# Weighing two score groups at once: eight passes in a row, with a ring of four groups of exponentials

## The chip, the cores and the metric

One core of one Trainium2 chip runs the kernel. The metric is the device time of one execution in microseconds (us). The kernel before took 2647.45 us (median of 3 runs, 2641.01 to 2655.77).

## The reference

The input is x, 8 batches of 1024 tokens with 512 features, all in float32. One layer is computed:

```python
Q, K, V = x @ W_Q.T, x @ W_K.T, x @ W_V.T            # 16 heads of 32 features
attn = where(causal, einsum('bhqd,bhkd->bhqk', Q, K) / sqrt(32), -inf)
y = einsum('bhqk,bhkd->bhqd', softmax(attn), V) @ W_O.T
x = layernorm(x + y)
p = softmax(x @ router_w.T + router_b)               # 8 experts
out = (x @ expert_w[argmax p].T + expert_b[argmax p]) * max(p)
x = layernorm(x + out)
```

## The kernel before, in words

**Stages.** `split_weights` splits the weights and the first batch of x into a high and a low part (fp32r), so that a product can be made of three passes. `attend` then does eight batches: seven in a hardware loop, the last one written out again. `run_experts` gathers the routed rows tile by tile and applies the experts. The change lies in `attend` alone.

**A batch.** An opening makes queries and keys of unit 1 and the row maxima of unit 0. Then come four units `u` of four heads each; a unit has 12 score groups `j` (`SCORE_GROUPS`), numbered through the batch as `n = 12 u + j`. A group is one block of 128 keys against one half (`BANK` = 512) of the queries, for four heads. Groups 0 to 3 belong to the first half and groups 4 to 11 to the second; because of the causal mask their widths are 512, 384, 256, 128 and 512 five times, 384, 256, 128 columns. Groups 0 to 3 and 8 to 11 lie on the diagonal. A closing makes the output products, the first layer norm, the routing, and queries, keys and values of the next batch.

**A group on each engine.** TensorE writes one score tile for each head (line 1009) into a ring of PSUM banks: 2 banks in units 0 and 1, 3 in unit 2, 4 in unit 3 (`score_bank`). ScalarE takes the exponential of each tile (line 697) into the SBUF ring `probs`, of `PROBS` = 3 groups. On the diagonal GpSimd zeroes the masked part (line 568). TensorE then weighs the group: `weigh(n, False)` multiplies it with the values into `y_ps`, `weigh(n, True)` with ones into `den_ps`, the sums. A weighing is four matmuls with 32 columns of weights, one for each head, side by side in the array by `tile_position`; each of them is two records in the trace, so that a weighing of a group is two passes over its columns, and both weighings together four passes. `weigh(n, True)` counts `probs_used`, which frees the slot of the ring. Below, a burst is a run of such passes between two full-width matmuls.

**The order on TensorE** is written out by hand, from line 1085 on. In each group the four score tiles stand with, between them, the row-maximum tiles of the next unit (`max_tile`, line 997; up to group 9 in unit 0, up to group 8 in units 1 and 2) and, in units 0 and 1, thirds of a projection for the unit after the next (line 951). Right after the second score tile of group n, group n - 2 (`LAG` = 2) is weighed:

```python
if n >= LAG and h == 1:
    weigh(n - LAG, False)
    weigh(n - LAG, True)
```

The last two groups of a batch are weighed after the loop. In unit 3 an output product of 12 matmuls follows groups 8, 9 and 10. `transpose_max` (line 1040) turns the finished maxima at the end of group 10 in unit 0 and of group 9 in units 1 and 2; ScalarE negates them and sends them by DMA into the query stack, where the score tiles of the next unit read them.

**VectorE** reduces the maximum tiles (lines 751 and 757) from a ring of three banks (four in unit 0's own opening), makes the low parts of projections, and copies `y_ps` and `den_ps` out when a half of a unit is weighed (`copy_y`, line 782, and `turn_sums`, line 790, at groups 2 and 6 of the unit).

**SyncE's queue** (`one_pass` of `block.sync`) issues the DMAs in a fixed order, each behind the waits of those before. `send(b, u)` sends the parts of unit u to its stacks and behind each of queries and keys loads the `w_qk` weights of the unit after (line 435). `load_xt(b + 1, 0)` and `(b + 1, 1)`, the first two parts of the next batch of x into `xt_raw` (line 439), are issued early in the batch, before `send(b, 2)`. ScalarE reads them in unit 2 (`split_high`, line 629, at groups 1, 3, 5, 7); GpSimd makes the low parts (`split_low`, line 525, at groups 4, 4, 6, 11), and parts 2 and 3 are loaded only when parts 0 and 1 have been split. In the closing `xt_raw` serves again, as `x_in`, for the residual (`load_x`, line 462).

Of the kernel before, what the change touches and what calls it, by code (L numbers as in the profile page):

```python
# [43 lines left out]
SETS = 3  # L44
PROBS = 3
LAG = PROBS - 1
WO_SET, WV_SET = 1, 2
# [101 lines left out]
def attend(nc, region_end, xt, xt_raw, x_t, x_rows, router_w_t, router_b, w_qk_parts, w_vo, dispatched):  # L149

    with ExitStack() as ctx:
# [11 lines left out]


        w_qk = sb("w_qk", [P, 2, 2, KT, P], F32R)
        q_st = [sb(f"q_stack{s}", [P, 4, SEQ], F32R) for s in range(SETS)]
        k_st = [sb(f"k_stack{s}", [P, 4, SEQ], F32R) for s in range(SETS)]
        v = sb("v", [P, ROWT, D])
        parts = sb("parts", [P, 2, 2, BANK], F32R)
        probs = sb("probs", [P, 4 * PROBS, BANK])  # L170
        rows = sb("rows", [P, ROWT, ROW])
# [165 lines left out]
        def weighed(eng, b, n):  # L337

            eng.wait_ge(probs_used.sem, probs_used.at(b, n))

        def scored(eng, b, n):

            eng.wait_ge(exp_done.sem, exp_done.at(b, 4 * n))
# [86 lines left out]
        def _(sp):  # L430
# [14 lines left out]
            def send(b, u):  # L445
                for o in (Q, K):
                    for t in range(HALVES):
                        send_tile(sp, b, u, o, t, range(SP_BLOCKS), sp_in, held_sp)
                    if not (u == UNITS - 1 and isinstance(b, int)):
                        load_w((u + 1) % UNITS, o)  # L450

# [7 lines left out]
            def one_pass(b, last):  # L459
# [10 lines left out]
                hold(sp, held_sp)  # L470
                for k in range(0 if last else 2):
                    load_xt(b + 1, k)
                wait_job(sp, b, proj_full, ("v", 6))
# [7 lines left out]
                send(b, 3)  # L481
                hold(sp, held_sp)
                scored(sp, b, GROUPS * 2)
                hold(sp, held_sp)
# [18 lines left out]
                for tb in range(2, ROWT):  # L503
                    wait_job(sp, b, proj_free, ("o", tb - 2))
                    load_x(tb)
                if not last:
                    send(b, 0)
# [6 lines left out]
        def _(pool):  # L514
# [43 lines left out]
            def one_pass(b, last):  # L558
                def keep_causal(u, j):

                    t, kb = SCORE_GROUPS[j]
                    n = GROUPS * u + j
                    c = column(kb, t)
                    for h in (0, 2):
                        pool.wait_ge(exp_done.sem, exp_done.at(b, 4 * n + h + 2))
                        hold(pool, held_pool)
                        block = probs[:, 4 * (n % PROBS) + h:4 * (n % PROBS) + h + 2, c:c + P]
                        nc.gpsimd.affine_select(out=block, in_=block, compare_op=ALU.is_ge, fill=0.0, base=0,  # L568
                                                pattern=[[0, 2], [1, P]], channel_multiplier=-1)\
                            .then_inc(probs_masked.sem, 1)  # L570
# [55 lines left out]
        def _(act):  # L626
# [25 lines left out]
            def one_pass(b, last):  # L652
# [29 lines left out]
                for u in range(UNITS):  # L682
                    for j, (t, kb) in enumerate(SCORE_GROUPS):
# [10 lines left out]
                        for h in range(4):  # L694
                            c = column(kb, t)
                            act.wait_ge(score_full.sem, score_full.at(b, 4 * n + h + 1))
                            nc.scalar.activation(probs[:, 4 * (n % PROBS) + h, c:BANK], score_bank(u, 4 * j + h)[:, c:BANK],  # L697
                                                 ACT.Exp, scale=SCALE).then_inc(exp_done.sem, 1)
                            if u + 2 < UNITS and h == 1:
                                for i in tiles_made(j):  # L700
                                    high(b, u + 2, i)
# [225 lines left out]
        def _(pe):  # L927
# [50 lines left out]
            def one_pass(b, last):  # L978
# [34 lines left out]
                def weigh(n, sums_too):  # L1013
# [13 lines left out]
                    for h in range(4):  # L1027
                        head = 4 * u + h
                        mm = nc.tensor.matmul((den_ps if sums_too else y_ps)[DH * h:DH * (h + 1), c:BANK],  # L1029
                                              ones_f[:, :] if sums_too else v[:, kb, head * DH:(head + 1) * DH],  # L1030
                                              probs[:, 4 * (n % PROBS) + h, c:BANK], start=kb == 0, stop=last,
                                              tile_position=(0, DH * h), skip_group_check=True)
                    if sums_too:
                        mm.then_inc(probs_used.sem, 1)

                def transpose_max(u):
# [52 lines left out]
                for u in range(UNITS):  # L1089
                    for j in range(GROUPS):  # L1090
# [8 lines left out]
                        for h in range(4):  # L1099
                            for i in share(maxed, h):  # L1100
                                max_tile(u + 1, i)
                            score_tile(u, j, h)
                            if h % 2 == 0:
                                for p in made[h // 2:h // 2 + 1]:
                                    project(b, u + 2, p // 3, third(p % 3))
                            if n >= LAG and h == 1:
                                weigh(n - LAG, False)
                                weigh(n - LAG, True)
                        if u == 0 and j == 0:
# [7 lines left out]
                        if u + 1 < UNITS and j == MAX_GROUPS[u > 0][1]:  # L1117
                            transpose_max(u + 1)
                for n in range(UNITS * GROUPS - LAG, UNITS * GROUPS):
                    weigh(n, False)  # L1120
                    weigh(n, True)

# [400 lines left out]
```

## Time and profile before

| what | value |
|---|---|
| median of 3 runs | 2647.45 us |
| the profiled execution | 2662.11 us |
| its span (first to last instruction) | 2660.4 us |
| mean granted TensorE clock | 0.964 of full speed |
| TensorE matmul busy | 2400.2 us, 90% |
| VectorE / ScalarE / GpSimd busy | 1451.5 / 1019.4 / 877.3 us |

The durations below come from the profiled execution; the median of the runs is 14.7 us under its time. Times of a row are microseconds from the start of its span. All rows of a stretch come from the fourth batch, whose unit 0 begins at 969.44, unit 1 at 1022.44, unit 2 at 1074.48 and unit 3 at 1119.25. A group's time is that from its first score matmul to the next group's.

### The profile page before, as it was taken

The page shows a single profiled execution, that of the slowest core. Times are in us where ns is not written, and L with a number is a line of the kernel's source. Part 1 is how long each engine was busy: PE and PEld are TensorE (multiplying, and loading weights), DVE is VectorE, ACT ScalarE, POOL GpSimd, SP SyncE. Part 2 cuts the span into 40 slices and gives each one's busy share as a digit, 9 for nine tenths or more (in the row PEclk, how much of TensorE's full clock was granted, in tenths as well). Part 3 has the DMA queues.
Part 4 walks back from the last instruction along what each step waited for, and adds up shares of the span by engine and source line. Part 5 has one row for each costly group of instructions (what it writes and reads, how often), then busy time and mean ns, then how long its engine had stood idle before and what let it go on. Part 6 is the DMA issues. An engine that isn't in the chain of part 4 may idle for free. (4 is left out here: it accounts for less than half of the span.)

```text
span 2660.4 us, 51133 instructions
## 1 busy us (share of the span) xinstructions
PE 2400.2 (90%) x14336; PEld 1534.2 (58%) x14337; DVE 1451.5 (55%) x3931; ACT 1019.4 (38%) x2089; POOL 877.3 (33%) x1531
## 2 busy tenths in 40 slices
PE   2999989999999989998999999999999899809998
PEld 1654665557554755476545755476547654607886
DVE  2576356734664367535663557437653675336665
ACT  2245414551345224531454144523452245223333
POOL 2222332323223232323223323232332322234656
PEclk9999999999999999998999999999999999859999
DMA  8432153314431253215231443134322421054443
GB/s 295 134 90 74 64 151 94 108 57 125 123 97 61 74 160 78 101 46 157 76 99 61 134 110 101 64 117 127 88 73 72 144 73 48 25 196 142 147 148 122
DMA packets 131032, 283.03 MB, mean 106 GB/s; under 512 B 33026, under 2 KB 42242, under 8 KB 128452
## 3 DMA queue, kind: packets, MB, share of 16 engines
q1 hardware_dynamic: 100920, 208.62, 26.0%
q0 software_dynamic: 28304, 70.64, 9.0%
q8 instruction: 124, 2.03, 0.3%
q14 instruction: 148, 1.21, 0.1%
q10 hardware_dynamic: 1536, 0.53, 0.1%
HBM read 133.04 MB, written 47.53 MB: 68 GB/s over the span
## 5 line engine op out<-in xcount | busy, mean ns | idle before, releaser
L697 ACT ACTIVATE probs<-score 128x512 f32<-128x512 f32 (+3 forms) x1216 | 561.8, 493 | 554.1 <-PE score L1009 538.4
L951 PE MATMUL proj<-xt,w_qk 128*128 128x512 f32 x1536 | 444.9, 405 | 59.1 <-DMA w_qk<-w_qk_parts 49.7
L568 POOL TENSOR_SCALAR_AFFINE_SELECT probs<-probs 128x256 f32<-128x256 f32 x512 | 218.5, 429 | 823.9 <-ACT probs L697 821.9
L1009 PE MATMUL score<-q_stack,k_stack 97*128 97x512 f32 (+2 forms) x1216 | 424.2, 372 | 16.3 <-ACT probs L697 16.2
L757 DVE CUSTOM_DVE_ANT_0 maxp<-maxp,mask_qk 128x384 f32<-128x384 f32 (+3 forms) x696 | 322.0, 506 | 207.1 <-PE maxp L997 201.3
L997 PE MATMUL maxp<-k_stack,q_stack 96*128 96x512 f32 (+2 forms) x1024 | 343.0, 378 | 41.1 <-DVE tile_max L757 14.7
L951 PEld LDWEIGHTS proj<-xt,w_qk 128*128 128x128 f32 x1536 | 287.5, 193 | 114.1 <-DMA w_qk<-w_qk_parts 49.4
L1029 PE MATMUL y_ps<-probs,v 128*32 128x512 f32 (+3 forms) x3072 | 332.9, 506 | 6.7 <-DVE rows L782 5.8
L1029 PE MATMUL den_ps<-probs,ones_f 128*32 128x512 f32 (+3 forms) x3072 | 322.8, 492 | 0.0
L1009 PEld LDWEIGHTS score<-q_stack,k_stack 97*128 97x128 f32 x1216 | 225.9, 190 | 127.3 <-ACT probs L697 81.4
L997 PEld LDWEIGHTS maxp<-k_stack,q_stack 96*128 96x128 f32 x1024 | 182.7, 191 | 198.1 <-DVE tile_max L757 75.6
L751 DVE TENSOR_REDUCE tile_max<-maxp 128x1 f32<-128x512 f32 x328 | 219.0, 684 | 58.8 <-PE maxp L997 55.6
L426 POOL DMA_DIRECT2D k_stack<-parts x256 | 126.2, 499 | 321.6 <-DVE parts L738 252.2
L1468 PE MATMUL ye_ps<-weight,xt_tile 128*128 x864 | 214.4, 397 | 0.0
L964 PE MATMUL proj<-q_stack,xt 128*128 128x512 f32 x768 | 209.5, 415 | 1.3 <-DMA rb<-router_b 1.3
L738 DVE TENSOR_TENSOR parts<-proj,parts 128x512 fp32r<-128x512 f32 x128 | 88.2, 689 | 199.5 <-ACT parts L640 175.5
L1052 PE MATMUL proj<-q_stack,parts 128*128 128x512 f32 x768 | 191.7, 399 | 5.7 <-DVE rows L808 3.4
L1029 PEld LDWEIGHTS den_ps<-probs,ones_f 128*32 128x32 f32 x3072 | 99.5, 111 | 155.0 <-issue 125.4
L1468 PEld LDWEIGHTS ye_ps<-weight,xt_tile 128*128 128x128 f32 x864 | 164.0, 190 | 36.1
L640 ACT ACTIVATE parts<-proj 128x512 fp32r<-128x512 f32 x128 | 76.2, 595 | 279.0 <-PE proj L951 227.9
L964 PEld LDWEIGHTS proj<-q_stack,xt 128*128 128x128 f32 x768 | 154.2, 202 | 33.4 <-DMA rb<-router_b 1.8
L1052 PEld LDWEIGHTS proj<-q_stack,parts 128*128 128x128 f32 x768 | 141.6, 189 | 40.1 <-issue 7.0
(144 smaller groups left out, 2872.6 us busy)
## 6 DMA issues: line engine op xcount, KB each, us to landing
w_qk<-w_qk_parts SPq DMA_DIRECT2D x64, 512.0 KB, 3.5
q_stack<-w_vo_parts SPq DMA_DIRECT2D x16, 2048.0 KB, 8.3
q_stack<-parts SPq DMA_DIRECT2D x512, 64.0 KB
k_stack<-parts SPq DMA_DIRECT2D x512, 64.0 KB
got<-dispatched SPq DMA_DIRECT2D x75, 257.0 KB, 2.6
xt_raw<-x_t SPq DMA_DIRECT2D x32, 512.0 KB, 4.1
q_stack<-parts POOLq DMA_DIRECT2D x256, 64.0 KB, 2.2
k_stack<-parts POOLq DMA_DIRECT2D x256, 64.0 KB, 2.1
```

Source lines behind the costliest of these rows:

```text
L426: eng.dma_start(dst[DH * block_row:DH * (block_row + 1), h, t * BANK:(t + 1) * BANK].bitcast(F32), parts[DH * h:DH * (h + 1), t, part, :]. ...
L568: nc.gpsimd.affine_select(out=block, in_=block, compare_op=ALU.is_ge, fill=0.0, base=0, pattern=[[0, 2], [1, P]], channel_multiplier=-1)\
L697: nc.scalar.activation(probs[:, 4 * (n % PROBS) + h, c:BANK], score_bank(u, 4 * j + h)[:, c:BANK], ACT.Exp, scale=SCALE).then_inc(exp_done ...
L751: nc.vector.tensor_reduce(tile_max[:, j, heads[0]:heads[0] + 1, qb], bank[:, 0:cols], AX.X, ALU.max)\
L757: top = nc.vector.tensor_tensor_reduce(out=tile, in0=tile, in1=mask_qk[:, BANK - cols:BANK], scale=1.0, scalar=-3.0e38, op0=ALU.add, op1=A ...
L951: mm = nc.tensor.matmul(proj[bank][:, :], w_qk[:, o, ws, k, :], xt[:, xs, k, t * BANK:(t + 1) * BANK], start=c == 0, stop=c == 3 * KT - 1)
L964: mm = nc.tensor.matmul(proj[bank][:, :], xt[:, xs, k, tb * P:(tb + 1) * P], wv[:, ws, k, :], start=c == 0, stop=c == 3 * KT - 1)
L997: mm = nc.tensor.matmul(bank[:, place * cols:to], q_st[u % SETS][0:3 * DH, h, qb * P:(qb + 1) * P], k_st[u % SETS][0:3 * DH, h, j * BANK:j ...
L1009: nc.tensor.matmul(score_bank(u, i)[:, c0:BANK], k_st[u % SETS][0:3 * DH + 1, h, kb * P:(kb + 1) * P], q_st[u % SETS][0:3 * DH + 1, h, t * ...
L1029: mm = nc.tensor.matmul((den_ps if sums_too else y_ps)[DH * h:DH * (h + 1), c:BANK], ones_f[:, :] if sums_too else v[:, kb, head * DH:(hea ...
L1052: mm = nc.tensor.matmul(bank[:, :], parts[:, tb % 2, ys, g * P:(g + 1) * P], wo[:, ws, g, :], start=c == 0, stop=c == 3 * UNITS - 1)
L1468: mm = nc.tensor.matmul(y_ps[s][:, :], xt[:, s % 2, xs, k * P:(k + 1) * P], weight[:, ws, bass.ds(e * (KT * D) + k * D, D)], start=False, ...
```

## The change

`PROBS` becomes 4 and `LAG` stays 2 (for VectorE's order). TensorE weighs nothing in even groups; in odd groups from n = 3 on, after the second score tile, `weigh_two(n - 3)` does the values of groups n - 3 and n - 2 and then the sums of both. After the loop `weigh_two(46)` takes the last two. The fourth slot of the ring lies in `xt_raw` for n below 20 and from there on in `probs_late`, which has the same place as `w_qk`. So that both are idle then, SyncE loads the first two parts of the next x after `send(b, 3)` and after group 19 has been weighed, and unit 0's `w_qk` not behind `send(b, 3)` but in the closing, after all groups are weighed.

```diff
-PROBS = 3
-LAG = PROBS - 1
+PROBS = 4
+LAG = 2
@@ attend
+        with nc.sbuf_tensor("probs_late", [P, 4, BANK], F32) as probs_late:
+            pass
         w_qk = sb("w_qk", [P, 2, 2, KT, P], F32R)
-        probs = sb("probs", [P, 4 * PROBS, BANK])
+        probs = sb("probs", [P, 4 * (PROBS - 1), BANK])
+        probs_early = xt_raw[:, :, :].rearrange("p k n -> p (k n)").rearrange("p (h n) -> p h n", n=BANK)
+        PROBS_EARLY = 5 * PROBS
+        def probs_of(n):
+            slot = n % PROBS
+            if slot < PROBS - 1:
+                return probs[:, 4 * slot:4 * slot + 4, :]
+            return probs_early if n < PROBS_EARLY else probs_late
@@ send of block.sync
-                    if not (u == UNITS - 1 and isinstance(b, int)):
-                        load_w((u + 1) % UNITS, o)
+                    if u + 1 < UNITS:
+                        load_w(u + 1, o)
@@ one_pass of block.sync
                 wait_last_batch(sp, b, proj_free)
                 hold(sp, held_sp)
-                for k in range(0 if last else 2):
-                    load_xt(b + 1, k)
                 wait_job(sp, b, proj_full, ("v", 6))
...
                 send(b, 3)
                 hold(sp, held_sp)
+                if not last:
+                    weighed(sp, b, PROBS_EARLY)
+                    hold(sp, held_sp)
+                    for k in range(2):
+                        load_xt(b + 1, k)
                 scored(sp, b, GROUPS * 2)
...
                 for tb in range(2, ROWT):
                     wait_job(sp, b, proj_free, ("o", tb - 2))
                     load_x(tb)
+                    if tb == QUARTER and not last:
+                        weighed(sp, b, UNITS * GROUPS)
+                        hold(sp, held_sp)
+                        load_w(0, Q)
+                        load_w(0, K)
@@ block.gpsimd keep_causal, block.scalar, block.tensor weigh: probs[...] becomes probs_of(n)[...]
@@ one_pass of block.tensor
+                def weigh_two(n):
+                    for sums_too in (False, True):
+                        weigh(n, sums_too)
+                        weigh(n + 1, sums_too)
...
-                            if n >= LAG and h == 1:
-                                weigh(n - LAG, False)
-                                weigh(n - LAG, True)
+                            if n >= PROBS - 1 and n % 2 and h == 1:
+                                weigh_two(n - PROBS + 1)
...
-                for n in range(UNITS * GROUPS - LAG, UNITS * GROUPS):
-                    weigh(n, False)
-                    weigh(n, True)
+                weigh_two(UNITS * GROUPS - 2)
```

## Rows read from the trace of the kernel before

**Rows 1.** The page's first part: each engine's busy time and share of the span.

```profile
PE 2400.2 (90%) x14336; PEld 1534.2 (58%) x14337; DVE 1451.5 (55%) x3931; ACT 1019.4 (38%) x2089; POOL 877.3 (33%) x1531
```

**Rows 2.** Timeline, PE, unit 0: start us, us, engine, line, out<-in, shapes, count.

```profile
1000.97 0.40 PE L997 MATMUL proj<-k_stack,q_stack 96*128 96x512 f32 x1
1001.21 0.40 PE L1009 MATMUL score<-q_stack,k_stack 97*128 97x512 f32 x1
...
1002.60 0.40 PE L1009 MATMUL score<-q_stack,k_stack 97*128 97x512 f32 x1
1002.93 1.07 PE L1029 MATMUL y_ps<-probs,v 128*32 128x512 f32 x8
1003.81 1.04 PE L1029 MATMUL den_ps<-probs,ones_f 128*32 128x512 f32 x8
1004.79 0.50 PE L997 MATMUL maxp<-k_stack,q_stack 96*128 96x512 f32 x1
1005.13 0.40 PE L1009 MATMUL score<-q_stack,k_stack 97*128 97x512 f32 x1
```

**Rows 3.** Pairs of groups: stretch, its length, busy PE PEld DVE ACT POOL, PEclk, DMA.

```profile
1006.36:1014.68 8.32, 8.32 (x50) 3.62 (x49) 6.91 (x18) 4.13 (x8) 3.63 (x7) 1.00 0.54 151
1030.60:1040.47 9.87, 9.72 (x64) 5.96 (x64) 8.39 (x20) 3.23 (x10) 4.05 (x8) 1.00 0.35 81
1049.47:1060.14 10.67, 10.67 (x62) 5.86 (x61) 7.47 (x17) 5.05 (x10) 1.97 (x4) 1.00 0.32 79
1080.21:1088.24 8.03, 7.29 (x52) 3.56 (x51) 7.27 (x19) 3.48 (x11) 1.93 (x5) 1.00 0.13 56
1097.33:1106.76 9.43, 9.43 (x50) 3.81 (x50) 4.17 (x12) 5.34 (x11) 1.34 (x1) 0.82 0.01 2
1128.13:1131.96 3.83, 3.83 (x42) 2.06 (x41) 0.43 (x1) 3.17 (x8) 0.41 (x1) 1.00 0.04 16
1131.96:1138.17 6.21, 6.21 (x41) 2.26 (x41) 2.54 (x5) 4.39 (x10) 0.00 (x0) 1.00 0.01 3
```

**Rows 4.** Timeline of unit 2: two reductions, two exponentials in a row; passes at half clock.

```profile
1085.38 1.28 DVE L751 TENSOR_REDUCE tile_max<-maxp 128x1 f32<-128x512 f32 x2
...
1075.01 1.09 ACT L697 ACTIVATE probs<-score 128x512 f32<-128x512 f32 x2 [0.42 <-PE score L1009]
...
1098.30 1.94 PE L1029 MATMUL y_ps<-probs,v 128*32 128x512 f32 x8
1100.00 1.71 PE L1029 MATMUL den_ps<-probs,ones_f 128*32 128x512 f32 x8
```

**Rows 5.** Timeline, from unit 0's last maxima to unit 1.

```profile
1013.42 0.50 PE L997 MATMUL proj<-k_stack,q_stack 96*128 96x512 f32 x1
...
1016.64 0.16 DVE L770 TENSOR_TENSOR row_max<-tile_max 128x16 f32<-128x16 f32 x1
...
1017.84 0.27 PE L1040 MATMUL proj<-ident,row_max 128*32 128x128 f32 x1
...
1021.92 0.68 PE L997 MATMUL maxp<-k_stack,q_stack 96*128 96x256 f32 x4 [1.05 <-DMA q_stack<-neg_max]
```

**Rows 6.** Timeline, unit 2, groups 4 and 5: who ended the stop of PE.

```profile
1089.02 4.73 POOL L525 TENSOR_TENSOR xt<-xt_raw,xt 128x1024 fp32r<-128x1024 f32 x2
...
1091.64 2.69 SPq L439 DMA_DIRECT2D xt_raw<-x_t  x2
...
1095.16 1.06 ACT L629 ACTIVATE xt<-xt_raw 128x1024 fp32r<-128x1024 f32 x1 [2.49 <-DMA xt_raw<-x_t]
...
1096.76 0.50 PE L1009 MATMUL proj<-q_stack,k_stack 97*128 97x512 f32 x1 [2.08 <-ACT probs L697]
```

**Rows 7.** Timeline, PE and PEld, the last weighings of the batch.

```profile
1157.03 0.64 PE L1029 MATMUL y_ps<-probs,v 128*32 128x256 f32 x8
1157.49 0.61 PE L1029 MATMUL den_ps<-probs,ones_f 128*32 128x256 f32 x8
1158.09 0.43 PE L1029 MATMUL y_ps<-probs,v 128*32 128x128 f32 x8
...
1158.09 0.16 PEld L1029 LDWEIGHTS y_ps<-probs,v 128*32 128x32 f32 x8 [0.47 <-POOL probs L568]
```

**Rows 8.** DMA issues (KB each, us to landing), then the timeline beside the moved loads.

```profile
w_qk<-w_qk_parts SPq DMA_DIRECT2D x64, 512.0 KB, 3.5
...
xt_raw<-x_t SPq DMA_DIRECT2D x32, 512.0 KB, 4.1
...
1063.85 0.58 SPq L435 DMA_DIRECT2D w_qk<-w_qk_parts  x1
...
1078.12 1.06 ACT L629 ACTIVATE xt<-xt_raw 128x1024 fp32r<-128x1024 f32 x1
...
1182.86 3.01 PE L951 MATMUL proj<-xt,w_qk 128*128 128x512 f32 x12
```

More of the change, by code:

```diff
@@ L566, in keep_causal @@
                         hold(pool, held_pool)
-                        block = probs[:, 4 * (n % PROBS) + h:4 * (n % PROBS) + h + 2, c:c + P]
+                        block = probs_of(n)[:, h:h + 2, c:c + P]
                         nc.gpsimd.affine_select(out=block, in_=block, compare_op=ALU.is_ge, fill=0.0, base=0,
@@ L696, in one_pass @@
                             act.wait_ge(score_full.sem, score_full.at(b, 4 * n + h + 1))
-                            nc.scalar.activation(probs[:, 4 * (n % PROBS) + h, c:BANK], score_bank(u, 4 * j + h)[:, c:BANK],
+                            nc.scalar.activation(probs_of(n)[:, h, c:BANK], score_bank(u, 4 * j + h)[:, c:BANK],
                                                  ACT.Exp, scale=SCALE).then_inc(exp_done.sem, 1)
@@ L1030, in weigh @@
                                               ones_f[:, :] if sums_too else v[:, kb, head * DH:(head + 1) * DH],
-                                              probs[:, 4 * (n % PROBS) + h, c:BANK], start=kb == 0, stop=last,
+                                              probs_of(n)[:, h, c:BANK], start=kb == 0, stop=last,
                                               tile_position=(0, DH * h), skip_group_check=True)
```

## The prediction

> **What bounds the kernel now.** I read the page's busy times first. TensorE (PE) has 90% and no other engine over 55% [rows 1]. That points at PE, but an end of a matmul is modelled, so I then read start times. In the timeline a full-width tile of 512 columns starts 0.24 us before the next (1000.97 to 1001.21 [rows 2]). Around a weighing it is different. From score tile to first pass it is 0.33 us. From the values to the sums, two passes, it is 0.88 us, but from the sums, also two passes, to the next full-width matmul 0.98. That matmul is 0.34 us ahead of its follower [rows 2]. So a burst costs 0.09 + 0.10 + 0.10, about **0.30 us**, above its passes, and none of this is a wait for another engine. Last come the stretches of two groups with each engine's busy time. They show where PE has company: VectorE (DVE) is busy for 7.27 of 8.03 us in groups 2 and 3 of unit 2, and for 8.39 of 9.87 in those of unit 1 [rows 3]. There a gain on PE is not surely a gain in time.
>
> The page TensorEngine Tiling of the Trainium skill says (Key Properties) that a change of the tiling mode drains the engine. That rule agrees with the 0.30 us and, read alone, gives the whole of the saving below. A rule of the same page speaks against the change: tiling makes TensorE faster, not the emptying of PSUM (PSUM Bottleneck). It would put the time near the rival "starved" below, which is priced there by rows.
>
> **Bursts removed.** In a batch groups 2 to 47 have a burst each, and the last two weighings stand together already: 47 bursts. Afterwards there is one in each odd group from 3 to 47 and the last: 24. That is 23 fewer per batch, 184 in all. The passes stay the same in number and width. 184 x 0.30 = 55 us is the gross saving. What of it becomes time, I take pair by pair (even and odd group), as the new burst lies in the odd one. The test for a pair is this. A burst now lasts 4 x 0.88 + 0.1 = 3.6 us for two groups of 512, against 1.9 for one. In it no new maximum tile is made. DVE lives on the three banks of its ring: two reductions in a row took 1.28 us, so three take 1.9 [rows 4]. That just covers a burst of 1.9 us. In the new one DVE stands still for about 1.7 us (1.3 where the second group has 384 columns). So the pair can't be shorter than DVE's busy time plus this idle time.
>
> - **Unit 0.** Groups 2 to 7 have room: -0.3 for each of three pairs. Groups 8 and 9: 6.91 + 1.7 = 8.6 against 8.32 now [rows 3], +0.3. Groups 10 and 11 lose both bursts' cost and more. Today the transposed maxima leave PE at 1017.84 and unit 1 begins 4.1 us later, after 1.05 us of idle PE that waited for the DMA of the maxima [rows 5]. From the end of group 9's burst (1013.42) to unit 1 it is 8.5 us. With no burst in group 10 PE reaches the transpose early and waits for DVE, which was done at 1016.8 [rows 5], 3.4 us after that burst. The burst of group 11 (3.2 us) and four score tiles (0.7) then fill the 4.1 us of the chain: 3.4 + 4.1 + 0.1 = 7.6, so -0.9. Sum: -1.5.
> - **Unit 1.** Groups 2 and 3: 8.39 + 1.3 = 9.7 against 9.87, -0.2. Groups 6 and 7: 7.47 + 1.7 = 9.2, under 10.67 [rows 3], so PE sets the time: -0.3. In the other four likewise -0.3 (pairs 0-1 and 4-5 have narrow bursts, the last two no maxima at their end). Sum: -1.7.
> - **Unit 2.** Groups 2 and 3: 7.27 + 1.3 = 8.6 against 8.03 [rows 3], +0.5. Groups 4 and 5 hold a stop that PE doesn't make: GpSimd (POOL) splits x from 1089.02, the next part is loaded at 1091.64, ScalarE (ACT) has it at 1095.16, and PE goes on at 1096.76 after 2.08 us [rows 6]. What PE saves before it, it waits there: 0. After the stop the granted clock is at its lower level, 1.2 GHz: 0.82 of full speed as a mean over groups 6 and 7 [rows 3], and the values' two passes take 1.70 us where they took 0.88 [rows 4, 2]. The new order has no burst in group 6; score and maximum tiles lie in that slow stretch, which wait for ACT and DVE anyway. I take 0.8 of the lost 1.7 us as saved, the middle, and -0.3: -1.1. The other three -0.3 each. Sum: -1.5.
> - **Unit 3** has no maxima but a balance of PE and ACT. Two exponentials in a row took 1.09 us, so a tile costs 0.49 [rows 4] and a group of 512 about 2.0. Groups 4 and 5 need 3.9 of ACT, as long as they last now (3.83 [rows 3]): +0.1. Groups 6 and 7: ACT has four banks, 2.0 us of work, in a burst of 3.6, so 3.9 + 1.6 + some 0.5 of restarting = 6.0 against 6.21 [rows 3]; I count 0 for it. Groups 0 and 1: -0.1. Groups 2, 3 and 8, 9: -0.3 each. At the end one burst less, but the values of group 47 now come before the sums of 46. That weighing waited for POOL's mask even today (0.60 from 46's sums to 47's values, against 0.46 from its values to its sums), and loses a cover of 0.46 [rows 7]: -0.3 + 0.4. Sum: -0.5.
>
> **-5.2 us per batch, -42 in all.**
>
> **The moved loads** I cost at nothing; this is their cover. The first two parts of x (2 x 512 KB, 4.1 us to landing) come behind `send(b, 3)`, which ends with the load at 1063.85 today, and behind group 19, weighed in group 9 of unit 1, near 1067. ACT wants part 0 at 1078.12 [rows 8]: some 7 us of room. The waiting SyncE queue holds back only the load of the output weights, which waits for the end of unit 1 anyway. Unit 0's `w_qk` (two loads, 3.5 us) comes just after the last weighing (near 1159) and is used at 1182.86 [rows 8]; of the residual's loads it stands ahead of those whose banks come free later. If a cover were gone, it would cost up to 4.1 us a batch, 33 in all. The fourth slot takes waits away rather than adding one: the exponentials of group n need group n - 4 weighed, which PE does before the scores of n. `y_ps` is wanted one group later after VectorE's copy. GpSimd's queue isn't changed.
>
> The profiled execution took 2662.1 us, so it would be 2620. The median of the runs lies 14.7 us under it: 2647.45 - 42 = **2606 us**.
>
> **Rivals.** *All of it* (chance 0.22): the stops of DVE and ACT are taken up by idle time elsewhere, 55 us, and with the end of unit 0 (0.6 x 8) and the slow clock (up to 1.7 x 8) 55 + 5 + 14 = 74: 2573 to 2592. For it: in most pairs DVE isn't busy for over 80%. Against it: the two pairs that are [rows 3]. *Absorbed* (0.13): the longer burst empties all rings, and only the 14 narrow or late pairs gain, 14 x 0.3 x 8 = 34, while the nine wide ones of units 0 to 2 lose 0.4 each (half of what I give groups 2, 3 of unit 2 and 8, 9 of unit 0, and the same again for ACT), 29: near 2642. *Starved, slower* (0.06): as *absorbed*, but DVE is what sets the time in all nine wide pairs of units 0 to 2, so that each takes on the whole 1.7 us of idle DVE in place of its 0.3. That is 9 x 1.4 x 8 = 101 against the remaining 14 x 0.3 x 8 = 34: 2647 + 67 = 2714. It decides where DVE's busy time plus 1.7 is over the pair's length now: 3 of the 9 are near it, and with 4 of 9 starved (4 x 1.4 = 5.6 a batch against 19 x 0.3 = 5.7) the sum is zero. *Not what it says* (0.06): the cost is one of each change of weights from values to sums, or the passes of the second group are kept waiting by its mask, so that as much is lost inside a burst as between two: 2647. Against it: inside a burst the passes of values and sums follow each other at 0.88 us for two. The forecast has 0.53.
>
> A measurement of this kernel can tell about 0.5% (13 us) from no change. Faster by more than that: the forecast, *all of it*, and some of *absorbed*, 0.83. Within it 0.11, slower 0.06. The range, 2578 to 2636, leaves out the far end of *all of it* and the three rivals on the other side.
>
> **What the new profile would show.** y_ps and den_ps rows of x16 in bursts near 3.6 us, 24 in a batch. Full-width starts at 0.24 us as before. DVE idle 1 to 2 us in the burst of each wide pair. Groups 2 and 3 of unit 2 longer than 8.03 us, those of the end of unit 0 shorter than 7.8. In unit 2 the stop for x still there and 2 us long. PE waiting for no load of x or `w_qk`. It is wrong if the unit times add up to less than 3 us of gain, if a burst holds an inner gap over 0.1 us as a rule, or if PE waits on the moved loads.

## The result: 4.4% slower, and the profile after

The changed kernel takes 2766.58 us (median of 4 runs, 2758.69 to 2779.54) where the kernel before took 2651.61 in the same series. The ratio is 1.0439, with a 95% interval of 1.0401 to 1.0476: **115 us slower**, where 2606 us was forecast, with a range up to 2636.

The page of the changed kernel: busy time of each engine, and the span in 40 slices (granted clock in tenths, TensorE busy in tenths).

```profile
span 2756.9 us, 51154 instructions
PE 2449.5 (89%) x14336; PEld 1572.9 (57%) x14337; DVE 1445.6 (52%) x3931; ACT 1010.2 (37%) x2089; POOL 874.0 (32%) x1531
PE   2998989999999989898989999999999998817998
PEclk9999999999999999999999999999999999958999
```

Work is the same in count [rows 1], VectorE's and ScalarE's busy time didn't grow, TensorE's did by 49 us. The clock says why: its mean granted share is 0.944 against 0.964, and the lower of its two levels is half of full speed. (1 - 0.944) x 2756.9 = 154 us of full speed are lost to the lower level now, (1 - 0.964) x 2660.4 = 96 us before: **59 us**. That is of the 96.5 us between the two profiled spans (2756.9 and 2660.4), not of the 115 between the medians. Clock that is lost while TensorE stands costs nothing, but counted over its busy time alone the two losses are 115 and 55 us, so the difference is the same. The drains saved are 184 x 0.30 = 55 us by the forecast's own price. So waits must have grown by about 96.5 + 55 - 59 = **93 us**, an estimate.

Where, I read from the score matmuls: the time from the first one of an even group to the first one of the next, as median of the eight batches, in both traces, beside the forecast's own terms. The last pair of unit 3 ends with the first output product behind it.

| pair | unit 0: before, change (forecast) | unit 1 | unit 2 | unit 3 |
|---|---|---|---|---|
| 0, 1 | 5.90, 0.0 (0) | 8.17, -0.3 (-0.3) | 5.74, +0.4 (-0.3) | 3.89, 0.0 (-0.1) |
| 2, 3 | 10.06, -0.3 (-0.3) | 9.87, -0.4 (-0.2) | 8.03, **+2.6** (+0.5) | 4.99, +0.3 (-0.3) |
| 4, 5 | 10.02, -1.0 (-0.3) | 9.00, -0.5 (-0.3) | 9.17, -0.1 (0) | 3.83, +0.2 (+0.1) |
| 6, 7 | 10.92, -0.3 (-0.3) | 10.66, -0.3 (-0.3) | 9.34, -1.7 (-1.1) | 6.21, +0.5 (0) |
| 8, 9 | 8.35, **+3.3** (+0.3) | 8.15, **+3.8** (-0.3) | 6.85, **+3.4** (-0.3) | 11.41, **+1.7** (-0.3) |
| 10, 11 | 7.72, +0.7 (-0.9) | 6.18, +0.8 (-0.3) | 5.65, +0.9 (-0.3) | 9.08, +0.1 (+0.1) |

Together +13.6 us a batch, 109 in eight. The rest of the closing, with the moved loads, didn't grow (93.8 before, 92.5 after). Groups 8 and 9 of units 0 to 2 alone are +10.4. The stretches of the fourth batch of the changed kernel, with the columns of [rows 3]: groups 4, 5 of unit 0, which gained; groups 8, 9 of units 0, 1 and 2; groups 2, 3 of unit 2 (fourth line).

```profile
1018.69:1027.67 8.98, 8.98 (x66) 6.79 (x65) 7.62 (x23) 4.60 (x9) 2.92 (x7) 1.00 0.43 124
1038.29:1049.94 11.65, 10.34 (x51) 4.06 (x50) 6.85 (x18) 4.07 (x8) 3.63 (x7) 0.85 0.35 94
1094.57:1107.07 12.50, 10.66 (x47) 3.71 (x46) 5.64 (x15) 4.12 (x9) 3.35 (x7) 0.73 0.21 47
1120.19:1130.83 10.64, 9.38 (x52) 4.06 (x51) 7.95 (x20) 3.47 (x11) 1.63 (x4) 0.84 0.07 30
1147.55:1157.81 10.26, 8.59 (x47) 3.24 (x45) 5.56 (x15) 3.41 (x9) 1.53 (x3) 0.83 0.00 0
```

The four stretches that lost here show a clock of 0.73 to 0.85; in [rows 3] groups 8, 9 of unit 0 and groups 2, 3 of units 1 and 2 had 1.00. Not every loss has that: groups 8 and 9 of unit 3 took 13.10 us at a clock of 1.00. The timeline of the second line, groups 8 and 9 of unit 0, TensorE with the VectorE instructions that matter:

```profile
1038.86 0.25 DVE L814 RECIPROCAL inv<-sums 128x16 f32<-128x16 f32 x1
1039.14 0.71 DVE L816 STREAM_TRANSPOSE sums<-inv 128x512 f32<-128x512 f32 x1
1039.39 0.48 PE L1028 MATMUL score<-q_stack,k_stack 97*128 97x512 f32 x1
1039.89 0.69 DVE L820 TENSOR_TENSOR rows<-rows,sums 128x512 f32<-128x512 f32 x1
1040.50 0.56 DVE L776 CUSTOM_DVE_ANT_0 maxp<-maxp,mask_qk 128x384 f32<-128x384 f32 x1
...
1041.17 0.50 PE L1016 MATMUL maxp<-k_stack,q_stack 96*128 96x512 f32 x1 [1.30 <-DVE tile_max L776]
...
1043.73 1.94 PE L1048 MATMUL y_ps<-probs,v 128*32 128x512 f32 x8
1045.44 1.59 PE L1048 MATMUL y_ps<-xt_raw,v 128*32 128x512 f32 x8
1046.85 1.03 PE L1048 MATMUL den_ps<-probs,ones_f 128*32 128x512 f32 x8
1047.71 1.03 PE L1048 MATMUL den_ps<-xt_raw,ones_f 128*32 128x512 f32 x8
1048.67 0.50 PE L1016 MATMUL proj<-k_stack,q_stack 96*128 96x512 f32 x1
```

Three things are to be seen. VectorE does the division of the unit's first half (`divide`, three instructions, 1.65 us) right before the maximum tiles of group 8. TensorE, which has no burst in group 8 any more, runs out of maximum banks and stands for 1.30 us. Then the burst starts at half clock: its first two passes take 1.71 us (1043.73 to 1045.44), the last two before a switch 0.86 (1046.85 to 1047.71). The burst lasts 4.94 us where 3.6 was forecast.

In some batches the clock stayed at its full level, and they tell the two losses apart. Groups 8 and 9 of unit 0 in the changed kernel's sixth batch, then groups 10 and 11 of unit 0 in its seventh and in its fourth:

```profile
1631.16:1641.19 10.03, 8.72 (x51) 3.73 (x50) 6.84 (x18) 4.07 (x8) 3.63 (x7) 1.00 0.41 110
1940.23:1947.02 6.79, 5.86 (x47) 2.83 (x46) 1.98 (x8) 2.85 (x10) 1.62 (x4) 1.00 0.02 6
1049.94:1058.40 8.46, 7.57 (x46) 3.18 (x46) 1.95 (x8) 2.86 (x10) 1.66 (x4) 0.80 0.02 5
```

At full clock groups 8 and 9 take 10.03 us in unit 0 and 9.74 in unit 1 (same batch): the wait costs 1.7 and 1.6 us over before, the clock another 1.6 and 2.2. In unit 2 no batch of this kernel shows it, but five of kernel 6 below do, with 8.57 us: 1.7 for the wait and 1.7 for the clock.

### The profile page after: what moved, and what is told of

It reads as the page before. It is cut to its first block and busy times, and to the rows that moved or that the text cites. A ratio compares the mean times of both kernels' runs of the same rounds, so it can differ in the third digit from the quotient of the medians.

```text
span 2756.9 us, 51154 instructions
## 1 busy us (share of the span) xinstructions
PE 2449.5 (89%) x14336; PEld 1572.9 (57%) x14337; DVE 1445.6 (52%) x3931; ACT 1010.2 (37%) x2089; POOL 874.0 (32%) x1531
## 3 DMA queue, kind: packets, MB, share of 16 engines
q14 instruction: 148, 1.21, 0.1%
## 5 line engine op out<-in xcount | busy, mean ns | idle before, releaser
L716 ACT ACTIVATE probs<-score 128x512 f32<-128x512 f32 (+2 forms) x912 | 448.8, 528 | 326.1 <-PE score L1028 317.7
L1028 PE MATMUL score<-q_stack,k_stack 97*128 97x512 f32 (+2 forms) x1216 | 437.2, 381 | 29.4 <-ACT probs L716 28.0
L587 POOL TENSOR_SCALAR_AFFINE_SELECT probs<-probs 128x256 f32<-128x256 f32 x384 | 165.2, 434 | 695.4 <-ACT probs L716 691.6
L1048 PE MATMUL y_ps<-probs,v 128*32 128x512 f32 (+2 forms) x2304 | 282.4, 597 | 0.0
L1048 PE MATMUL den_ps<-probs,ones_f 128*32 128x512 f32 (+2 forms) x2304 | 253.1, 542 | 0.0
L1048 PEld LDWEIGHTS den_ps<-probs,ones_f 128*32 128x32 f32 x2304 | 79.3, 118 | 146.1 <-issue 146.1
```

The lines of the kernel that those rows point to most:

```text
L716: nc.scalar.activation(probs_of(n)[:, h, c:BANK], score_bank(u, 4 * j + h)[:, c:BANK], ACT.Exp, scale=SCALE).then_inc(exp_done.sem, 1)
L1028: nc.tensor.matmul(score_bank(u, i)[:, c0:BANK], k_st[u % SETS][0:3 * DH + 1, h, kb * P:(kb + 1) * P], q_st[u % SETS][0:3 * DH + 1, h, t * ...
```

## The experiments

Before's time is that of the same series of runs each time; the ratio and its 95% interval are those on record, up to 0.23% from the quotient of the two medians. Kernel N is that of experiment N. "One by one" means the order of before (values and sums of group n - 2 in group n).

**1. The ring and the loads alone.**

```diff
-                            if n >= PROBS - 1 and n % 2 and h == 1:
-                                weigh_two(n - PROBS + 1)
+                            if n >= LAG and h == 1:
+                                weigh(n - LAG, False)
+                                weigh(n - LAG, True)
```

(and the same after the loop).

> The ring of four, its slot in idle buffers and the moved loads alone; each group is weighed by itself, two groups behind, as before. Theory (idle TensorE before long bursts lowers its clock, and VectorE and ScalarE stand still in the bursts): the loads and the ring cost nothing, so 2640 to 2660 us, ratio to before 0.995 to 1.005. Rival (the moved loads or the fourth slot are late somewhere and hold TensorE): most of the 115 us lost stands here too, 2700 us or more.

Measured 2645.38 us against 2645.1, ratio 0.9998 (0.9978 to 1.0018). Nothing of the loss is in the ring, its borrowed buffers or the moved loads.

**2. Another order within the burst.** `weigh_two` does values and sums of n, then of n + 1.

> The changed kernel with the eight passes in another order: values and sums of the first group, then values and sums of the second. Same bursts at the same places. Theory (what is lost lies between the bursts and in the clock, not in the order of the passes): 2755 to 2780 us as the changed kernel. Rival (the second group's values right behind the first's wait for weights or mask): 20 to 60 us faster than the changed kernel.

Measured 2759.57 us, ratio 1.0423 (1.04 to 1.0447); the changed kernel's 1.0439 lies within it. The loss is not in the order of the passes.

**3. More work on TensorE.**

```diff
+                def filled(u, j):
+                    return j == 8 and 0 <= u < UNITS - 1 or j == 2 and u == 2
@@ max_tile, around the matmul
+                        for _ in range(1 + filled(u - 1, group_of)):
@@ score_tile, around the matmul
+                    for _ in range(4 if j == 10 and u < UNITS - 1 else 1 + filled(u, j)):
```

> The changed kernel with more work on TensorE: the maximum and score tiles of group 8 in units 0 to 2 and of group 2 in unit 2 are multiplied twice, the score tiles of group 10 in units 0 to 2 four times, into the same bank before it is given on (the values don't change). Theory (the clock falls because TensorE stands idle in these groups since their burst left, and the 3.6 us burst behind them then runs at 1.2 GHz): half-clock time falls from about 300 us towards 200, the passes in groups 3, 9 and 11 come back to 0.43 us each, and the time falls by 20 to 60 us although work was added. Rival (a long burst itself lowers the clock, or the loss is only the waiting for VectorE): half-clock time stays near 300 us, and the time stays or grows by up to 30 us.

Measured 2730.56 us, ratio 1.0315 (1.0293 to 1.0336): 36 us faster than the changed kernel for more matmuls, and a mean clock of 0.962, which puts the time at half clock at 207 us (2 x 0.038 x 2728.5) where the changed kernel has 309. Its timeline of groups 8 and 9 of unit 0:

```profile
1031.37 0.74 PE L1020 MATMUL maxp<-k_stack,q_stack 96*128 96x512 f32 x2 [0.33 <-DVE tile_max L776]
...
1034.14 1.06 PE L1055 MATMUL y_ps<-probs,v 128*32 128x512 f32 x8
1035.03 1.04 PE L1055 MATMUL y_ps<-xt_raw,v 128*32 128x512 f32 x8
1035.89 1.04 PE L1055 MATMUL den_ps<-probs,ones_f 128*32 128x512 f32 x8
1036.74 1.04 PE L1055 MATMUL den_ps<-xt_raw,ones_f 128*32 128x512 f32 x8
1037.72 0.50 PE L1020 MATMUL proj<-k_stack,q_stack 96*128 96x512 f32 x1
```

The wait is 0.33 us in place of 1.30, filled with useless products, and the same burst runs at full clock: 0.85 to 0.89 us for two passes, 3.58 in all. That the clock has a share in the loss is shown; the time that VectorE needs stays, filled in part with added products (the pair still takes 10.32 us, 8.35 before).

**4. Two at once where it paid.**

```diff
+        def paired(n):
+            u, j = divmod(n, GROUPS)
+            return n >= PROBS - 1 and (j in (1, 5, 7) or u < 2 and j == 3)
...
+                                if n % 2 and paired(n):
+                                    weigh_two(n - PROBS + 1)
+                                elif n >= LAG and not paired(n + 1 - n % 2):
+                                    weigh(n - LAG, False)
+                                    weigh(n - LAG, True)
```

> Two groups at once only where the trace of the changed kernel shows a gain or little loss: the bursts in groups 1, 5 and 7 of every unit and in group 3 of units 0 and 1; all others (groups 2, 3 of units 2 and 3, groups 8 to 11) are weighed one by one as before. 13 of the 23 removals per batch stay. Theory (a removed burst is worth 0.3 us where TensorE has other work in its place, and costs where it hasn't): 13 x 0.3 x 8 = 31 us under before, less what VectorE and ScalarE take back: 2615 to 2640 us, ratio 0.987 to 0.997. Rival (the switch saves nothing that reaches the end): 2650 us or more.

Measured 2628.9 us, ratio 0.9929 (0.9902 to 0.9955), **0.7% faster than before**: 16 us by the medians, 19 by the ratio. Groups 8 and 9 of units 0 to 2 are back at 8.34, 8.15 and 6.85 us, groups 2 and 3 of unit 2 at 8.02. Removed drains do reach the end. It gains less than 31 because groups 4, 5 (+0.2) and 6, 7 (+0.5) of unit 3 and groups 0, 1 of unit 2 (+0.4) lose what they lost in the changed kernel. Besides, this kernel and kernels 5 to 13 keep `weigh_two(46)` after the loop, behind single bursts. It saves no switch there and waits for the mask of group 47: the end of a batch takes 9.51 us in place of 9.08, 3.4 us in eight.

**5. Only the pairs that had gained.** Bursts for two in groups 3, 5, 7 of unit 0; 1, 3, 5, 7 of unit 1; 7 of unit 2.

> Two groups at once only where the traces so far show the pair of groups shorter than before: bursts in groups 3, 5, 7 of unit 0, groups 1, 3, 5, 7 of unit 1 and group 7 of unit 2; all other groups one by one. Theory: the gains of the hybrid kernel's pairs add up (unit 0: 0.3 + 1.0 + 0.3, unit 1: 0.3 + 0.4 + 0.5 + 0.3, unit 2: 0.4, together 3.5 us per batch), its losses (unit 2 groups 0, 1 and unit 3) are gone: 28 us under before, 2610 to 2625 us, ratio 0.987 to 0.992. Rival (the pairs aren't independent, what one gains the next waits for): no better than the hybrid kernel, ratio 0.993 or more.

Measured 2626.66 us over 6 runs, ratio 0.9921 (0.9902 to 0.9941). That is 2 us above the expected 2610 to 2625. In its trace the 24 stretches add up to 2.7 us a batch less than before, 22 in eight; the runs show 19 (interval of the ratio: 16 to 26), where 28 were expected. The gains of its eight pairs stand (3.5 us a batch), but the end of unit 0 takes 0.4 us more and the end of the batch too; that it is better than kernel 4 is within the intervals.

**6. The one burst that hurts, alone.** `paired(n)` is `j == 9 and u < UNITS - 1`.

> One by one as before, but for the burst of groups 6 and 7 in group 9 of units 0, 1 and 2. Three bursts fewer per batch than before. Theory (TensorE stands idle in group 8 waiting for VectorE, the clock falls, the 3.6 us burst runs at 1.2 GHz): this alone costs what groups 8 and 9 lost in the changed kernel, 3.3 + 3.8 + 3.4 us per batch, so 60 to 90 us over before. Rival (the loss needs the whole chain of long bursts): under 25 us over before.

Measured 2725.52 us, ratio 1.028 (1.0249 to 1.031). Three bursts fewer per batch cost 80 us: within the theory's range. Groups 8, 9 of units 0 to 2 take 12.1, 11.4 and 8.6 us. In unit 2 the longest wait is 1.5 us in every batch, and the clock stays full all the same in five of eight: such a wait doesn't lower it each time.

**7 and 8. Less work for VectorE around it, and the control.**

```diff
-                            reduce_tile(u + 1, i)
+                            reduce_tile(u + 1, i, j in (8, 9))
@@ reduce_tile(u, i, short=False)
+                    if short:
+                        cols = P
```

> The kernel with the burst in group 9 of units 0 to 2, but VectorE reads only 128 of the columns of the maximum tiles of groups 8 and 9 (the rest of those tiles is left out of the row maxima). Everything on TensorE stays. Theory (it is VectorE that TensorE waits for in group 8): the idle time in group 8 goes, with it the half clock of the burst; groups 8 and 9 are then 0.3 us or more shorter than with single bursts and the same short reductions, so 5 to 15 us under that kernel. Rival (TensorE waits there for ScalarE's exponentials, or the clock falls by the burst itself): it stays 50 us or more over it.

> The control: every group weighed by itself as before, with the same short reductions in groups 8 and 9. Theory: VectorE's work in these groups was covered by TensorE's single bursts, so 0 to 20 us under before.

Measured 2683.84 us (ratio 1.0131, 1.0104 to 1.0158) and, for the control with single bursts, 2651.77 (1.0022, 1.0003 to 1.0041), where 0 to 20 us under before was expected; 3.4 us of these 6 are the end of the batch (see experiment 4). 42 us of the 80 went, but the kernel is 32 us over its control where 5 to 15 under it was expected: VectorE's tile reductions were part of it, not all. Its timeline of unit 1 shows two waits left in group 8.

```profile
1072.58 0.69 DVE L827 TENSOR_TENSOR rows<-rows,sums 128x512 f32<-128x512 f32 x1
...
1073.53 0.76 PE L1023 MATMUL maxp<-k_stack,q_stack 96*128 96x512 f32 x2 [0.61 <-DVE tile_max L777]
...
1075.22 0.44 PE L1035 MATMUL score<-q_stack,k_stack 97*128 97x384 f32 x1 [0.51 <-ACT probs L721]
```

**9 and 10. Less work for ScalarE too, and its control.**

```diff
+                            if j == 8 and u < UNITS - 1:
+                                c = BANK - P
```

> As the kernel with the burst in group 9 and short reductions, and the exponentials of group 8 in units 0 to 2 are taken over 128 of their 512 columns only (the rest is left out). With short reductions alone TensorE still stood 1.4 to 1.7 us in group 8, 0.6 of it for VectorE and the rest in waits for ScalarE to empty a score bank. Theory (group 8 waits for both, and the two together are what idles TensorE and lowers the clock): now its waits fall under 1 us, hardly a burst in group 9 starts at half clock, and the time is 25 us or more under the 2684 of short reductions alone and 0 to 15 us under its own control. Rival (the long burst lowers the clock whatever stands before it): bursts in group 9 of units 0 and 1 still start at 0.85 us per set of passes, 30 us or more over the control.

> The control: every group weighed by itself, with short reductions in groups 8 and 9 and short exponentials in group 8. Theory: nothing there was on the path that sets the time, 2630 to 2655 us.

Measured 2688.78 us (ratio 1.0186, 1.014 to 1.0231) and 2646.71 (1.0036, 1.0011 to 1.0061): no gain over kernel 7, where 25 us or more were expected. The theory in this form fell. The burst of unit 1 now starts at full clock (0.45 us for its first set of passes, median of eight batches), that of unit 0 still at half (0.86). Unit 1's pair fell to 8.6 us (9.8 in kernel 7), but unit 0's rose to 10.9 (10.1): its clock fell in seven batches, in kernel 7 in four, behind a wait that was hardly longer (1.2 us, 1.0 in kernel 7). The trace showed what I had left in place: the division.

```profile
1016.99 0.78 DVE L829 TENSOR_TENSOR rows<-rows,sums 128x512 f32<-128x512 f32 x1
1017.69 0.28 DVE L785 CUSTOM_DVE_ANT_0 maxp<-maxp,mask_qk 128x128 f32<-128x128 f32 x1
...
1018.09 0.51 PE L1025 MATMUL maxp<-k_stack,q_stack 96*128 96x512 f32 x1 [1.21 <-DVE tile_max L785]
```

It ends at 1017.77; only then comes the next reduction, and TensorE has waited 1.21 us. Shortening what comes behind the division can't shorten this wait.

**11. The division later, all work whole.** In units 0 to 2 `divide(2 * u)` moves on VectorE from group 7 to group 10; the burst for two stays in group 9.

```diff
-                        if u < UNITS - 1 and j == HALF0 + LAG + 1:
+                        if u < UNITS - 1 and j == GROUPS - 2:
                             divide(2 * u)
```

> The kernel with the burst in group 9 of units 0 to 2, all work whole, and the division of a unit's first half (0.24 + 0.71 + 0.69 us on VectorE, which stands in its order before the maximum tiles of group 8) moved from group 7 to group 10 in units 0 to 2. Theory (TensorE's wait in group 8 is for a maximum bank, behind that division): the wait in group 8 falls by 0.5 to 1.5 us, and the time from 2725 to 2670 to 2705 us. Rival (the tile reductions alone fill VectorE): 2715 us or more.

Measured 2671.98 us against 2664.46 in this series (the chip of this series was slower): ratio 1.0024 (1.001 to 1.0039), where kernel 6 had 1.028. One move of three VectorE instructions takes back 2.6%, some 67 us by the ratios, at the far end of what I had expected. Groups 8 and 9 of unit 0, first kernel 6, then this one:

```profile
1031.72:1043.22 11.50, 10.19 (x50) 4.06 (x50) 6.84 (x18) 4.14 (x8) 3.60 (x7) 0.85 0.40 109
```

```profile
1009.65:1018.08 8.43, 8.43 (x50) 3.73 (x49) 5.32 (x15) 4.11 (x8) 3.22 (x7) 1.00 0.59 149
```

and the burst in this one, the same passes as in kernel 6, at full clock:

```profile
1013.25 1.06 PE L1053 MATMUL y_ps<-probs,v 128*32 128x512 f32 x8
1014.13 1.04 PE L1053 MATMUL y_ps<-xt_raw,v 128*32 128x512 f32 x8
1014.99 1.04 PE L1053 MATMUL den_ps<-probs,ones_f 128*32 128x512 f32 x8
1015.85 1.04 PE L1053 MATMUL den_ps<-xt_raw,ones_f 128*32 128x512 f32 x8
1016.82 0.50 PE L1021 MATMUL proj<-k_stack,q_stack 96*128 96x512 f32 x1
```

So a burst of 3.57 us does not by itself lower the clock: what differs is the waits before it, none in unit 0 and at most 0.36 us in the others, and the clock is full over groups 8 and 9 of units 0 to 2 in all eight batches. The pair takes 8.43 us, though, no less than before (8.35): the drain saved goes into what is left of the wait.

**12. All three at once.** Division late, short reductions, short exponentials.

> As the kernel with short reductions and short exponentials around the burst in group 9, with the division in group 10. With those two alone TensorE still waited 0.8 to 1.2 us in group 8 for a maximum bank, because of the division. Theory (waits in group 8 idle TensorE, and that sets the clock of the burst): waits in group 8 under 0.8 us, the bursts of units 0, 1 and 2 start at 0.45 us, and the time is 2630 to 2660 us, within 15 us of the control with single bursts (2647). Rival (the long burst is what lowers the clock): the burst of unit 0 still runs at 0.85 us per set, 2675 us or more.

Measured 2661.03 us, just over the 2630 to 2660 expected but in a slower series, ratio 0.9986 (0.9973 to 1.0), against 1.0036 for the control: 0.5% under it, each against before in its own series (the control has the division in its old place). All three long bursts start at 0.45 us in all units. The rival, that a long burst lowers the clock whatever stands before it, is out.

**13. The best version with the late division.**

> The kernel that weighs two at once only in groups 3, 5, 7 of unit 0, 1, 3, 5, 7 of unit 1 and 7 of unit 2 (2627 us), with the division in group 10. Theory: VectorE's division was covered there, so the same time, 2620 to 2632 us; if it held a tile back behind the burst of group 7, up to 10 us less.

Measured 2643.16 us against 2664.46, ratio 0.9921 (0.9903 to 0.9939): the same as kernel 5. The 2620 to 2632 us expected were worked out from a faster series; the ratio is as expected. The division costs nothing where a single burst covers it.

**14. The changed kernel with the late division.**

> The changed kernel with the division in group 10. Theory: of the 69 us of slow clock and 86 us of waits that the changed kernel has over before, the part of group 8 of units 0 to 2 shrinks: 2720 to 2750 us against 2767. Rival (the exponentials alone hold group 8): 2755 us or more.

Measured 2711.14 us against 2664.46, ratio 1.0178 (1.0151 to 1.0205), where the changed kernel has 1.0439; it is better than the 2720 to 2750 us expected. **This move undoes 2.6 of the 4.4%.** Groups 8 and 9 of units 0 to 2 are at 8.43, 8.13 and 6.93 us.

## Why the prediction was wrong

**The step that failed** is the test for a pair. It asked only what the doubled burst in the odd group does to VectorE ("the pair can't be shorter than DVE's busy time plus this idle time") and never what its absence in the even group does to TensorE. Two prices were missing.

*The wait.* A single burst in group 8 was 1.9 us of TensorE work beside VectorE's division and reductions. Without it TensorE waits there. In unit 1 I had booked -0.3 because "the last two [have] no maxima at their end", in unit 2 without a reason; the maxima of group 8 and the division in front of them were in the busy time of a row like unit 0's, but not their order in it. A busy share of 6.91 in 8.32 us [rows 3] doesn't say when. The test gave 8.6 us for that pair; with the clock at its full level it took 10.03. Kernels 7, 9, 11 and 12 show the parts of this wait: taking VectorE's tile work away gave 42 us, moving the division 67; the two overlap and don't add.

*The clock.* I priced the lower clock once, as a gain behind unit 2's stop for x. That term came, -1.7 for -1.1, but by luck: it was to come from a slow stretch that costs less without its burst, and in six of eight batches these groups ran at full clock (7.64 us), while in the sixth, at 0.68, they took 10.68, longer than before. Kernel 10, which leaves them as they were, has them at 8.12 against 9.34: the clock over them moved without a change in them. I had [rows 6] before me, a stop of TensorE followed by the half clock, and didn't ask what new waits would do. Here waits of up to 1.5 us, in units 1 and 2 several within a group, were followed by it in most batches, and the long burst stands right behind them. Such a burst of two groups of 512 took up to 5.9 us in place of 3.6 (kernel 6, unit 1). The change in the clock is 59 us of the 96.5 between the profiled spans. Kernel 3 (added work, 36 us less) and kernel 11 (same burst, other order on VectorE) show it. The Trainium skill, TensorE: Matmul & The Clock Gate, in its section on a second failure mode (PSUM queue cycling), says that in one kernel very short idle times of the engine between groups of matmuls came often enough to make its clock swing between its two levels. The trace agrees in that the longest single wait of unit 0's pair is 1.30 us and the clock 0.85 over it; the section does not explain that the same wait leaves the clock full in other batches. That page's rule was a rival that I should have had.

**Other terms.** *Drains:* the price is right. In bursts at full clock the passes follow at the forecast times (3.57 us against 3.6), and in kernel 5 seven of the eight pairs gain 0.28 to 0.46 us each. That its 19 us equal 8 x 0.30 x 8 is chance: the eighth, groups 4 and 5 of unit 0, gains 1.05 (forecast -0.3), and other places lose. There TensorE had waited 0.55 us for a maximum bank behind a narrow burst of 0.6 us, and behind the burst of two groups, 1.4 us, that wait is gone. In the kernel before, that wait is this row:

```profile
995.10 0.50 PE L997 MATMUL maxp<-k_stack,q_stack 96*128 96x512 f32 x1 [0.55 <-DVE tile_max L751]
```

*Groups 2, 3 of unit 2:* forecast +0.5, came +2.6, with a clock of 0.84 over the stretch; in the sixth batch, at full clock, they took 8.92 us, so 0.9 is the wait. Single bursts there (kernel 4) restored 8.02 us. *End of a unit:* forecast -0.9, -0.3, -0.3, came +0.7, +0.8, +0.9. In unit 0 it was the clock that I had missed: in the two batches where it was full the pair took 6.8 us, 0.9 less than before, as forecast, and in the six others, at 0.80, 8.4 to 8.5. In units 1 and 2 the clock was full (but for one batch), and what failed is the wait. I had counted on PE to reach the transpose early and wait only for VectorE. It waits for ScalarE too, since no burst separates the score tiles of group 10, in unit 1 for 0.87 us: ScalarE has to negate the maxima and issue their DMA before it takes the next exponentials. The changed kernel, unit 0, then unit 1:

```profile
1050.58 0.66 PE L1028 MATMUL score<-q_stack,k_stack 97*128 97x256 f32 x2 [0.26 <-ACT probs L716]
1051.44 0.38 PE L1028 MATMUL score<-q_stack,k_stack 97*128 97x256 f32 x1 [0.20 <-ACT probs L716]
1052.26 0.28 PE L1065 MATMUL proj<-ident,row_max 128*32 128x128 f32 x1 [0.43 <-DVE row_max L789]
...
1107.28 0.25 ACT L676 ACTIVATE neg_max<-proj 32x128 fp32r<-32x128 f32 x1
1107.57 0.53 ACTq L679 DMA_DIRECT2D q_stack<-neg_max  x1
1108.71 0.66 PE L1028 MATMUL score<-q_stack,k_stack 97*128 97x256 f32 x2 [0.87 <-ACT probs L716]
```

*Groups 8, 9 of unit 3:* forecast -0.3, came +1.7, with the clock full in six batches of eight. The first output product needs the low part of y, which GpSimd makes behind ScalarE's copy, after the exponentials of group 7. The burst of group 8 had covered that; now TensorE stands.

```profile
1185.10 1.15 ACT L691 ACTIVATE parts<-rows 128x512 fp32r<-128x512 f32 x2
1185.82 2.31 POOL L594 TENSOR_TENSOR parts<-rows,parts 128x512 fp32r<-128x512 f32 x2 [11.22 <-ACT parts L691]
1187.23 2.98 PE L1077 MATMUL proj<-q_stack,parts 128*128 128x512 f32 x12 [1.46 <-ACT probs L716]
```

The product begins right after the first of the two low parts (half of 2.31 us from 1185.82); the profile puts the wait down to an exponential. A single burst there gives the pair back its 11.38 us (kernel 4). *The tail:* +0.4 forecast for the mask of group 47; the step from 46's values to 47's is 1.06 us in the trace (1204.41 to 1205.47) where 0.46 are passes, a wait of 0.60 against 0.14 before [rows 7], so +0.46; the pair came at the forecast +0.1. *Moved loads:* nothing, as forecast (kernel 1).

**The rivals.** *Starved, slower* (2714 us) had the right sign and engine and some of the right places, and a chance of 0.06. Its point of decision was wrong as well: it counted idle time of VectorE in the burst, and it set 4 starved pairs of 9 as the limit, where three a batch with the clock behind them already cost 80 us (kernel 6).

**Open.** The 1.8% that remain in kernel 14 I place by the pairs (groups 10, 11; groups 2, 3 of unit 2; unit 3), and kernel 4 shows that single bursts there undo them, but no run tells the share of ScalarE and VectorE in each. The clock's share in all is on record: over the runs of that series its mean was 0.9505, and 0.9625 for before, which is 134 us lost against 100, so 34 of the 47 us. Open too is why the clock falls in one batch and not in the next behind the same wait.

## What to carry to other kernels

A piece of work on the busiest engine that looks like overhead may be the cover for another engine's backlog at that very place. Before moving it, list, for the place that it leaves, what each other engine does in order, and not only its busy share. Then batch such work only where the engine has something else to run: here 8 of the 23 mergings gave 0.8%, all 23 cost 4.4%. And price the clock with every new wait on TensorE: a long run of matmuls right behind the wait pays for it.

## What the runs showed that I had not expected

TensorE's granted clock fell to 1.2 GHz after waits of 0.2 to 1.0 us within a group, with matmuls between them (kernel 6, unit 1), and after a single one of 1.3 us (unit 0). It stayed at 2.4 GHz in all batches where the waits in that place were about 0.5 us or less (kernels 3, 11 and 12). It didn't fall each time: behind 1.5 us in unit 2 of kernel 6 it did in three batches of eight. Adding products whose results are thrown away made a kernel 36 us faster.
